# Expert loop of a cross-attention and mixture-of-experts kernel: from one tile per step to pairs of tiles

## What is computed

```python
x = x + tanh(g_xattn) * xattn(layernorm(x), ctx)
xf = layernorm(x)
probs = softmax(xf @ gate_w.T); top_p, top_i = top_k(probs, 2)
h1, h2 = xf @ expert_fc1[e].T, xf @ expert_fc2[e].T       # 256 -> 176, for every expert e
out_e = (silu(h1) * h2) @ expert_proj[e].T                # 176 -> 256
y = sum over the two chosen experts of combine[:, e] * out_e
shared = silu(xf @ shared_fc1.T) * (xf @ shared_fc2.T) @ shared_proj.T   # 256 -> 704 -> 256
x = x + tanh(g_ffn) * (y + sigmoid(xf @ shared_gate_w.T) * shared)
```

## Time and profile before

| | |
|---|---|
| three runs, median (range) | 312.28 us (312.01 to 313.63) |
| profiled execution, its own time | 312.68 us |
| its span | 310.9 us |
| PE busy | 278.3 us, 90% of the span |
| DVE busy | 216.4 us, 70% |
| ACT busy | 170.5 us, 55% |
| POOL busy | 128.8 us, 41% |
| mean granted TensorE clock | 0.991 of full speed |

### The profile page before, as it was taken

How to read it: one execution, slowest core, us unless ns; L and a number is a source line. 1 busy time by engine, 2 the same in 40 slices (tenths; PEclk the granted TensorE clock), 3 DMA queues, 4 the chain that set the end, 5 groups by cost and what they waited for, 6 DMA issues and landing times.

```text
span 310.9 us, 5835 instructions
## 1 busy us (share of the span) xinstructions
PE 278.3 (90%) x1783; PEld 247.5 (80%) x1783; DVE 216.4 (70%) x698; ACT 170.5 (55%) x399; POOL 128.8 (41%) x142
## 2 busy tenths in 40 slices
PE   0686989998998888799999999899999999999984
PEld 0555968887887777589888888799999999998863
DVE  2665667878978957756766776787787777754465
ACT  1547576786745645555234555466666666654220
POOL 0520351351486063743333000027777777775000
PEclk9999999999999999999999999999999999999996
DMA  6580215102027031443233656158888888765994
GB/s 212 203 257 14 60 25 174 65 18 104 1 76 274 0 108 42 126 159 118 100 105 107 203 189 204 45 158 137 138 133 137 138 138 137 118 69 65 290 359 163
DMA packets 30478, 40.18 MB, mean 129 GB/s; under 512 B 2928, under 2 KB 26608, under 8 KB 30448
## 3 DMA queue, kind: packets, MB, share of 16 engines
q1 hardware_dynamic: 22864, 30.05, 30.7%
q0 software_dynamic: 7152, 9.57, 18.4%
q10 hardware_dynamic: 432, 0.18, 0.3%
HBM read 22.68 MB, written 17.11 MB: 128 GB/s over the span
## 4 chain that ended last, share of the span: by engine, by line
PE 57%; DVE 20%; ACT 7%; DMA 7%; issue 5%; SPq 2%; POOL 2%; POOLq 0%; DVEq 0%; ACTq 0%
PE bank L406 42%; PE bank L629 8%; DVE ew_lo L954 4%; DMA ew_hi<-y_d 3%; ACT ew_hi L734 3%; PE bank L675 3%; PE bank L710 2%; DMA weight_stage<-wa_dram 2%; DVE xt_lo L954 2%; SPq L388 2%; DVE neg_max L994 2%; POOL y_d L1436 1%; DMA y_d<-work,dest_of_slot 1%; DVE work L1259 1%; ACT work L766 1%
## 5 line engine op out<-in xcount | busy, mean ns | idle before, releaser
L1436 POOL DMA_INDIRECT y_d<-work,dest_of_slot x39 | 60.6, 1553 | 57.0 <-DVE dest_of_slot L1331 55.4
L406 PE MATMUL bank<-ew_hi,xt_hi 128*128 (+2 forms) x172 | 53.8, 322 | 0.3 <-issue 0.3
L406 PE MATMUL bank<-ew_lo,xt_hi 128*128 (+2 forms) x172 | 51.8, 301 | 0.0
L406 PE MATMUL bank<-ew_hi 128*128 128x256 f32 (+1 forms) x100 | 32.3, 323 | 15.9 <-ACT ew_hi L734 14.1
L406 PE MATMUL bank<-ew_hi,xt_lo 128*128 (+1 forms) x133 | 40.5, 305 | 0.0
L954 DVE TENSOR_TENSOR xt_lo<-bank,xt_hi 128x256 fp32r<-128x256 f32 (+2 forms) x90 | 35.6, 397 | 2.7 <-ACT xt_hi L734 1.5
L1400 POOL DMA_INDIRECT xs_d<-xn_all,slot_of_pair x32 | 32.6, 1018 | 10.3 <-issue 7.3
L954 DVE TENSOR_TENSOR ew_lo<-bank,ew_hi 128x512 fp32r<-128x512 f32 (+1 forms) x41 | 22.6, 580 | 19.1 <-ACT ew_hi L734 18.9
L406 PEld LDWEIGHTS bank<-ew_hi 128*128 128x128 f32 x100 | 19.3, 193 | 19.9 <-ACT ew_hi L734 16.5
L406 PE MATMUL bank<-xt_hi,sw_hi 128*128 128x512 f32 x88 | 34.8, 396 | 0.0
L406 PE MATMUL bank<-xt_lo,sw_hi 128*128 128x512 f32 x88 | 34.5, 392 | 0.0
(11 more groups left out here) (156 smaller groups left out, 671.9 us busy)
## 6 DMA issues: line engine op xcount, KB each, us to landing
work<-xs_d SPq DMA_DIRECT2D x39, 136.0 KB, 2.5
weight_stage<-ew_dram SPq DMA_DIRECT2D x10, 486.5 KB, 3.7
ew_hi<-y_d SPq DMA_DIRECT2D x8, 512.0 KB, 7.7
y_d<-work SPq DMA_DIRECT2D x6, 512.0 KB, 3.2
xn_all<-x_dram SPq DMA_DIRECT2D x4, 512.0 KB, 5.1
work<-ctx_t_dram SPq DMA_DIRECT2D x4, 512.0 KB, 3.5
out_dram<-xn_all SPq DMA_DIRECT2D x3, 512.0 KB, 5.1
xs_d<-pad_row SPq DMA_DIRECT2D x9, 136.0 KB, 1.9
```

What stands on the lines that cost most here:

```text
L406: last = nc.tensor.matmul(dst, a, b, start=(n == 0), stop=(n == len(pairs) - 1))
L1436: nc.gpsimd.indirect_dma_start(out=y2_d, out_offset=bass.IndirectOffsetOnAxis(ap=IX[:, n:n + 1], axis=0), in_=EY[:, n % 4, :], in_offset=None,
```

## The change

The loop runs over 20 pairs of tiles (the last has one tile). In pair m PE does up(2m), up(2m+1), down(2m-2), down(2m-1), inner transposed (2m), (2m+1), rows transposed (2m+4), (2m+5). ACT and DVE follow in that order. The rows are transposed four tiles ahead in place of two: `EXT`, the transposed rows, now uses four places in place of two. Tiles 2 and 3 are transposed before the loop. As the order no longer implies that a bank is free, each part of PE waits for a second semaphore. After the last pair come half of the shared block, the last down, and the other half.

```diff
@@ PE
-            def xx(n, w, visit):
-                pe.wait_ge(d_ex[w], visit)
+            def xx(t):
+                pe.wait_ge(d_ex[t % 4], 16 * (t // 4) + 16)
+                at_least(pe, e_xl, t - 1)
                 for k in range(KD):
-                    last = nc.tensor.transpose(B[w % 2][:, k * P:(k + 1) * P], EX[:, w, k * P:(k + 1) * P], ident)
+                    last = nc.tensor.transpose(B[t % 2][:, k * P:(k + 1) * P], EX[:, t % 4, k * P:(k + 1) * P], ident)
                 last.then_inc(e_xx, 1)
+            def up(t):
+                pe.reg_load(expert[t % 4], EID[0:1, t:t + 1])
...
+                             [(EXT[a][:, t % 4, k, :], fcs[k][b]) for k in range(KD) for a, b in THREE],
+                             [(0, e_xl, t + 1), (0, e_h, t - 1)])
+                last.then_inc(e_fc, 1)
+            def down(t):
...
+                             [(0, e_hl, t + 1), (0, e_y, t - 1)])
+                last.then_inc(e_pj, 1)
+            def hx(t):
+                pe.wait_ge(e_h, t + 1)
+                at_least(pe, e_hl, t - 1)
...
+            def e_pair(m):
+                for t in tiles_of(m):
+                    up(t)
+                for t in tiles_of(m - 1):
+                    down(t)
+                if m == 0:
                     pe.wait_ge(v_z, 4 * PRE)
+                for t in tiles_of(m):
+                    hx(t)
+                for t in tiles_of(m + 2):
+                    xx(t)
             pj(0, 0)
             blocks(0, PRE, 3)
             pe.wait_ge(ew_lo, E_PIECES)
             pe.wait_ge(v_eid, 1)
-            e_steps(e_step)
-            pe.wait_ge(e_h, SLOT_TILES)
+            xx(2)
+            xx(3)
+            for m in range(PAIRS):
+                e_pair(m)
+            pe.wait_ge(e_xl, SLOT_TILES)
+            fc(PRE, 0, (0,))
+            for t in tiles_of(PAIRS - 1):
+                down(t)
+            fc(PRE, 0, (1,))
             blocks(PRE, N_CH, 1)
@@ ACT
+            for t in range(4):
+                rows_hi(t)
+            for m in range(PAIRS):
+                for t in tiles_of(m):
+                    silu(t)
+                for t in tiles_of(m - 1):
+                    result(t)
+                for t in tiles_of(m):
+                    inner_hi(t)
+                for t in tiles_of(m + 2):
+                    rows_hi(t)
+            for t in tiles_of(PAIRS - 1):
+                result(t)
@@ DVE
             nc.vector.memset(EH, 0.0)
-            e_step(-2, 2, -1)
-            e_step(-1, 3, -1)
+            for t in range(2):
+                rows_lo(t)
             s_sums(PRE - 1)
-            e_steps(e_step)
+            for t in range(2, 4):
+                rows_lo(t)
+            for m in range(PAIRS):
+                for t in tiles_of(m):
+                    gated(t)
+                for t in tiles_of(m):
+                    inner_lo(t)
+                for t in tiles_of(m + 2):
+                    rows_lo(t)
```

More of the change, by code:

```diff
@@ L258, in build, with tiles_of @@
         LAST_FIRST = (LAST,) + tuple(range(LAST))
[L260 to L269, removed]
+        PAIRS = (SLOT_TILES + 1) // 2
+        def tiles_of(m):
+            return [t for t in (2 * m, 2 * m + 1) if 0 <= t < SLOT_TILES]
         def pair(s, j):
@@ L372, in _ @@
                 load_tile(i)
-            def e_step(s, u, m):
+            for s in range(SLOT_TILES):
                 if s + 4 < SLOT_TILES:
@@ L657, in blocks @@
                         pe.wait_ge(v_h, 6 * PRE)
-                        xx(0, 0, 16)
-                        xx(1, 1, 16)
+                        xx(0)
+                        xx(1)
                     if n >= 2:
@@ L676, in xx @@
                 last.then_inc(e_xx, 1)
[L678 to L703, removed]
-                    pe.wait_ge(v_z, 4 * PRE)
[L705 to L721, removed]
@@ new lines, in up @@
+            def up(t):
+                pe.reg_load(expert[t % 4], EID[0:1, t:t + 1])
+                e = pe.snap(expert[t % 4], min_val=0, max_val=N_E - 1)
+                fcs = [[EFC[b][:, bass.ds(e * (KD * 2 * F_E) + k * 2 * F_E, 2 * F_E)] for b in range(2)] for k in range(KD)]
+                for ap in fcs[0] + fcs[1]:
+                    pe.lower_ap(ap)
+                last = chain(B[2 + t % 2][:, 0:2 * F_E],
+                             [(EXT[a][:, t % 4, k, :], fcs[k][b]) for k in range(KD) for a, b in THREE],
+                             [(0, e_xl, t + 1), (0, e_h, t - 1)])
+                last.then_inc(e_fc, 1)
@@ new lines, in down @@
+            def down(t):
+                e = pe.snap(expert[t % 4], min_val=0, max_val=N_E - 1)
+                pjs = [[EPJ[b][:, bass.ds(e * (2 * D) + m * D, D)] for b in range(2)] for m in range(2)]
+                for ap in pjs[0] + pjs[1]:
+                    pe.lower_ap(ap)
+                last = chain(B[6 + t % 2][:, 0:D],
+                             [(EHT[a][:, t % 2, 0, :], pjs[0][b]) for a, b in THREE]
+                             + [(EHT[0][0:TAIL_K, t % 2, 1, :], pjs[1][b][0:TAIL_K, :]) for b in range(2)],
+                             [(0, e_hl, t + 1), (0, e_y, t - 1)])
+                last.then_inc(e_pj, 1)
@@ new lines, in hx @@
+            def hx(t):
+                pe.wait_ge(e_h, t + 1)
+                at_least(pe, e_hl, t - 1)
+                for i in range(2):
+                    last = nc.tensor.transpose(B[4 + t % 2][:, i * P:(i + 1) * P], EH[:, t % 2, i * P:(i + 1) * P], ident)
+                last.then_inc(e_hx, 1)
+            def e_pair(m):
[4 more added lines that the diff above has]
+                if m == 0:
+                    pe.wait_ge(v_z, 4 * PRE)
+                for t in tiles_of(m):
+                    hx(t)
+                for t in tiles_of(m + 2):
+                    xx(t)
@@ L916, in _ @@
                             expert_weights(n)
[L918 to L934, removed]
-                    act.wait_ge(e_ix, s - 1)
-                    at_least(act, d_ey[(s - 2) % 4], (s - 2) // 4 * 16)
-                    copy(EY[:, (s - 2) % 4, :], B[6 + u % 2][:, 0:D], scale=WS[:, s - 2:s - 1]).then_inc(e_y, 1)
@@ L939, in _, with rows_hi, silu @@
-            act.wait_ge(p_fc, 6 * PRE)
-            e_step(-2, 2, -1)
-            e_step(-1, 3, -1)
-            e_steps(e_step)
+            def rows_hi(t):
+                act.wait_ge(e_xx, t + 1)
+                at_least(act, e_fc, t - 3)
+                copy(EXT[0][:, t % 4, :, :], B[t % 2][:, 0:D].rearrange("p (k n) -> p k n", k=KD)).then_inc(e_xh, 1)
+            def silu(t):
+                act.wait_ge(e_fc, t + 1)
+                at_least(act, e_h, t - 1)
+                nc.scalar.activation(ETH[:, t % 2, :], B[2 + t % 2][:, 0:F_E], ACT.Silu).then_inc(e_th, 1)
@@ new lines, in inner_hi, with result @@
+            def inner_hi(t):
+                act.wait_ge(e_hx, t + 1)
+                at_least(act, e_pj, t - 1)
+                copy(EHT[0][:, t % 2, :, :], B[4 + t % 2][:, 0:D].rearrange("p (m n) -> p m n", m=2)).then_inc(e_hh, 1)
+            def result(t):
+                act.wait_ge(e_pj, t + 1)
+                act.wait_ge(e_ix, t + 1)
+                at_least(act, d_ey[t % 4], t // 4 * 16)
+                copy(EY[:, t % 4, :], B[6 + t % 2][:, 0:D], scale=WS[:, t:t + 1]).then_inc(e_y, 1)
```

40 lines of the change are left out of this document (18 added, 22 removed).

## The result

The changed kernel takes 318.5 us (median of 6 runs, 317.19 to 321.62) against 312.28 for the kernel before; the ratio of the runs is 1.0186, with a 95% interval of 1.0149 to 1.0224. It is slower, as forecast (317.4, range 313.2 to 320.0). The profiled execution took 318.0 us, 5.3 more than that of before.

A forecast was written before the change was run, and what follows sets the result against it. PE, never idle at 2.00 us per step, was taken to set the loop's pace. +1.5 us at the start, +3.0 in the loop and +0.2 at the end make +4.7 on 312.68: 317.4 us, range 313.2 to 320.0.

The forecast's parts named there:

- the prediction's reading: In PE's loop, a pair starts at the start of its second up matmul less 0.16 us.
- the array's pace: Rival: PE's array sets the loop's pace, 3.97 us a pair, total 313.6 us, +0.9; chance 0.22.
- point 4: Loop: ACT and DVE queueing puts the next pair's second `e_h` at F + 7.18; with 1.20 behind it, period 4.19 us.
- F: The start of a pair's first up on PE, from which the forecast counts its times.
- point 2: Loop: second `e_h` at F + 2.92 at the earliest holds PE's sequencer; next up 1.20 later, F + 4.12, not 3.97.
- Point 3: PE's extra waits between release and next up: three at 0.10 us, cancelled by 0.30 of address work; 1.20 kept.
- Point 5: Loop start: DVE's two more tiles of rows (1.02 us) put up(2) at 205.39, against 203.90 before.
- Point 6: Loop end: up(36) at 276.4; POOL limits the last additions at 1.86 us each, the last issued at 287.8.
- Point 7: Items without cost: extra `EXT` places, SP's loads issued two pairs ahead and landing in some 2.5 us, `d_ey`.
- The tail: From the landing of the last addition to `y2_d` to the span's end: 24.0 us, left as they are.
- Faster: Rival: grouping transposes saves more than 0.02 us; POOL allows at most -3.1, 309.6 us; chance 0.08.
- The change doesn't do what it says: Rival: the eight transposes aren't one group, as the second inner pair waits for `e_h`; gap under 0.1 us.

The follow-up runs named there:

- addresses early: Changed kernel with fewer waits on PE and the next pair's first register load and addresses put ahead of the inner transposes: 313.37 us, ratio 1.0040 to before.
- six more waits: Changed kernel with six long-satisfied waits added per pair between the inner and the rows' transposes: 322.72 us, ratio 1.0321 to before.
- the failed attempt to reorder DVE: Kernel with early addresses and eight load buffers, plus DVE doing the first pair's products ahead of rows of tiles 2 and 3: 314.13 us, ratio 1.0028.
- eight buffers: Changed kernel with eight buffers for the loaded rows in place of four and nothing else: 317.71 us, ratio 1.0183 to before.
- both edits: Changed kernel with fewer waits on PE, and the next pair's first register load and addresses ahead of the inner transposes: 316.15 us, ratio 1.0128 to before.

## Why the prediction was right, and where its terms were off

**The mechanism held.** "The sequencer is held until" the second `e_h`, and the next up comes some 1.1 to 1.3 us later. By the prediction's reading it is 233.47 to 234.75 = 1.28 in the pair shown, 229.39 to 230.48 = 1.09 one pair earlier, 204.31 to 205.55 = 1.24 at the start, and 1.15 in the mean of the 15 pairs (1.05 to 1.35); the forecast was 1.20. That the work behind the wait is what takes the pair above the array's pace is shown by addresses early, which takes only the register load and the address operations from there and gets 4.01. By the Trainium skill ("TensorE: Matmul & The Clock Gate", Part 2) weight loads are pulled ahead of running matmuls. The runs show that this does not reach past a register load that stands behind an unmet wait: the weight load at 234.64 comes after the register load at 233.9, with 0.24 us of idle time before it.

**The period.** Forecast 4.19 by point 4, measured 4.18 without the two long pairs. The steps of point 4 came out near: the first subtraction at F + 4.10 (230.37 with F = 226.27) where I had 4.09, the second `e_h` at F + 7.20 (233.47) where I had 7.18, twice the period 7.20 + 1.15 = 8.35 and not 8.38. The 7.20 holds to 0.04 in all pairs but three: the first (7.11) and those of the two long ones (8.12 and 7.77). It is not one even period, though: single pairs range from 4.03 to 4.31, mostly a short one after a long one. Points 2 and 4 together allow this. By point 4 a release hangs on the start of the pair before its own, so only the sum of two periods is fixed; these sums are 8.25 to 8.48. By point 2 no release can come sooner than 2.92 us after its own pair's start (measured 2.92 to 2.94 at the least), and 2.93 + 1.10 = 4.03 is the shortest pair. A part of it is in the way from release to up as well: in the pair shown the two waits at 233.52 and 233.80 are 0.28 apart, one pair earlier 0.13. What makes that step is open.

**Point 3, the waits.** I counted four between release and up, one of them in the 1.20 already, and took 0.10 for each of three. The trace has three, so two more than in step 1, and the kernel with six more waits prices one at 0.11; this is within my 0.05 to 0.13. Against it, the sequencer's address work takes 0.53 us in step 1 (203.23 to 203.76) and 0.19 in a pair (234.32 to 234.51), 0.34 less where I had set 0.30. So my 0.30 against 0.30 was 0.22 against 0.34, which is why the 1.15 is a little under 1.20.

**Point 5, the start.** +1.5 forecast, +1.65 measured, by another way than I gave: `e_h` of tile 1 came at 204.31 (forecast 204.19) because of the up matmuls, the silu and the product, not because of DVE's two extra tiles of rows; the failed attempt to reorder DVE shows it. That the two times agree is luck.

**Point 6, the end.** The saturation of POOL and its 1.86 us held. Up(36) came at 278.23, not 276.4, and the last issue at 289.59, not 287.8. The difference of 1.8 is nearly all in the next point.

**Point 7, the term that failed.** "SP's loads (issued two pairs ahead, they land in some 2.5 us)" stood under "without cost". They cost two pairs (5.20 - 4.18) + (4.84 - 4.18) = 1.7 us in this profile. Both halves of the sentence were off. The load was not issued two pairs, 8 us, ahead: SP waits for `e_ix` too, which DVE gives late in a pair. In the long pair tile 23's transposes ended at 243.07 and its indices at 245.39, the load into its buffer was asked for at 246.55, and its rows were needed at about 251.3, 4.75 us later. And it wasn't there. The median landing was the wrong row for a wait that every tile must pass: the latest of 39 loads decides. Of the 1.0 us that this pair lost, 0.46 is the wait for rows, and 0.28 is idle time for the sequencer's work, which stands behind that wait too. With eight buffers, in one profile, the last issue is 287.66, near the forecast's 287.8. `d_ey`, also under "without cost", cost nothing in the changed kernel, but in three of the others ACT waited once for an addition (0.3 to 0.5 us).

**The tail.** I said that 24.0 us would stay as they are. It was 22.9, which gave back 1.1 of the 1.8. In the other ten profiles it lies between 22.3 and 24.0, with no order by kernel: the profiled execution of before has a tail at the long end. In that execution the granted clock is 0.50, the level of 1.2 GHz, from 305.4 us to the end, after PE had been idle for 1.25 us before 305.0; the last ten matmuls take 2.50 us (305.71 to 308.21). In the changed kernel's the clock stays at 1.00 to 314.6, and they take 1.46 us (311.58 to 313.04). That is 1.0 us, but it doesn't settle the matter: the way from the landing to the last of the sums read is 15.9 us before and 12.2 after, and the rest differs in the other direction. So the close agreement of the total, 317.4 against 318.0 profiled, is partly two errors of opposite sign.

**The rivals.** The array's pace (313.6, chance 0.22; it is the first rival listed, though an earlier sentence of the prediction calls it the second) is what the kernel with addresses early has: 4.01 a pair and 313.37 us. It takes 0.81 us from release to up, where I had asked for under 0.76; with the measured 4.01 and 7.20 in place of 3.97 and 7.18 the bound is 0.82. Faster was excluded by the same number: grouping is worth nothing on the array. "The change doesn't do what it says" did not come to pass, the eight run as one group.

No version with pairs beat the kernel before. The best of them has its time (1.0003, interval 0.9977 to 1.0028).

## What to carry to other kernels

Look at what stands in program order behind each wait, not only at what the wait guards: a register load and address arithmetic behind a late semaphore come between its release and the next matmul each time, and here moving them ahead of the wait took a pair from 4.18 to 4.01 us. Waits that are already satisfied are free where the sequencer runs ahead and cost about 0.11 us for each wait instruction between a late release and the next use of what it frees; two of them can share one instruction. A load that comes late costs more than its lateness when register work stands behind the wait for it. When a reordering shortens the time between the request and the use of a load, compare the new distance with the slowest landing, not with the median.

## What was not expected of the hardware

A load of 136 KB lands in 2.3 to 2.7 us by the median, but now and then in over 5 (5.29 in the kernel with both edits, 5.13 with six more waits). By the packets of the trace, 15 of its 16 shares are in on time and one is 1 to 4 us behind. It happens in the kernel before too, where it is covered: there a load is asked for 5.05 to 5.51 us before its use, in the changed kernel 4.1 to 6.2. In the cases I looked at there was a fetch of instructions at the same time: in the kernel before, the two slowest of the loop's recorded loads were asked for at 217.5 (4.3 us) and 231.6 (3.5 us), and the fetches of 16 KB stand at 218.9 and 232.7. This is that queue's line in the changed kernel for 246 to 252 us, the first long pair (packets, MB, share of 16 engines):

```profile
q8 instruction: 1, 0.02, 1.0%
```

That the one makes the other late was not tried.
